# Contracting over 64 rows instead of 128 in the second score matmuls of a fused attention and mixture-of-experts kernel

## The reference: what is computed

```python
q = layernorm(x)                                     # 64 x 128 x 512, 32 heads of 16
scores  = einsum('bkgsd,bktd->bkgst', qh, kh) / 4.0  # kh, vh: the context, 8 heads of 16
weights = softmax(scores, axis=-1)
x = x + tanh(g_xattn) * einsum('bkgst,bktd->bkgsd', weights, vh)
```

## Time and profile before

| what | us |
|---|---|
| median of 3 runs | 2383.96 |
| lowest and highest run | 2383.93, 2397.22 |
| span of the profiled execution, first to last instruction | 2381.9 |
| mean granted TensorE clock over the span | 0.984 |
| first stage | about 0 to 715 |
| second stage | about 715 to 795 |
| third stage | about 795 to 2382 |

### The profile page before, as it was taken

The page is one execution under the profiler, slowest core; times in us unless marked ns, Lnnn a source line. Parts: engine busy times, 40 slices in busy tenths (PEclk is TensorE's granted clock), DMA queues, the critical chain, the costliest instruction groups (busy, mean ns, idle before and its releaser), DMA issues.

```text
span 2381.9 us, 41762 instructions
## 1 busy us (share of the span) xinstructions
PE 2290.9 (96%) x12545; PEld 1775.2 (75%) x12545; DVE 1144.9 (48%) x2214; ACT 815.7 (34%) x1426; POOL 589.5 (25%) x1378
## 2 busy tenths in 40 slices
PE   7999999999991699999999999999999999999998
PEld 5777777777771577777777777777777777777776
DVE  6999999999987422322323223232332223323232
ACT  6888888888883110101101011010110101101010
POOL 5666666666657100000000000000000000000000
PEclk9999999999995899999999999999999999999999
DMA  2444444444445422222222212322123221232211
GB/s 77 138 133 136 134 133 136 131 138 131 137 121 192 100 78 87 93 87 72 77 98 95 85 62 77 111 89 77 62 77 114 86 77 62 88 103 86 77 44 42
DMA packets 238538, 234.83 MB, mean 99 GB/s; under 512 B 88625, under 2 KB 164401, under 8 KB 238514
## 3 DMA queue, kind: packets, MB, share of 16 engines
q1 hardware_dynamic: 234162, 221.89, 29.8%
q0 software_dynamic: 4352, 12.65, 1.7%
HBM read 161.88 MB, written 71.57 MB: 98 GB/s over the span
## 4 chain that ended last, share of the span: by engine, by line
PE 66%; DVE 0%; DVEq 0%; issue 0%
PE acc L1053 7%; PE p_g L1066 7%; PE p_g L1068 7%; PE p_g L1067 7%; PE acc L1054 7%; PE acc L1055 7%; PE p_u L1068 7%; PE p_u L1067 7%; PE p_u L1066 7%; PE p_x L1096 2%; PE p_y L1083 2%; PE p_x L1083 2%; PE p_x L1074 0%; PE p_y L1089 0%; DVE keys L1036 0%; DVEq L848 0%
## 5 line engine op out<-in xcount | busy, mean ns | idle before, releaser
L997 DVE TENSOR_TENSOR act_f<-p_u,act_f 128x512 f32<-128x512 f32 x176 | 121.7, 691 | 1035.3 <-PE p_u L1068 1035.3
L968 ACT ACTIVATE act_f<-p_g 128x512 f32<-128x512 f32 x176 | 105.2, 598 | 1203.2 <-PE p_g L1068 1203.2
L530 DVE TENSOR_REDUCE negmax<-p_max 128x8 f32<-128x1024 f32 x256 | 313.1, 1223 | 66.5 <-PE p_max L672 52.0
L1053 PE MATMUL acc<-wd_h,hh 128*128 128x512 f32 x704 | 279.1, 396 | 0.0
L1066 PE MATMUL p_g<-xh,wgu_h 128*128 128x512 f32 x704 | 276.3, 392 | 1.3 <-PEq L721 1.3
L1068 PE MATMUL p_g<-xh,wgu_l 128*128 128x512 f32 x704 | 274.5, 390 | 0.0
L1067 PE MATMUL p_g<-xl,wgu_h 128*128 128x512 f32 x704 | 274.5, 390 | 0.0
L1054 PE MATMUL acc<-wd_l,hh 128*128 128x512 f32 x704 | 274.3, 390 | 0.0
L1055 PE MATMUL acc<-wd_h,hl 128*128 128x512 f32 x704 | 274.2, 390 | 0.0
L1068 PE MATMUL p_u<-xh,wgu_l 128*128 128x512 f32 x704 | 273.9, 389 | 0.0
L1067 PE MATMUL p_u<-xl,wgu_h 128*128 128x512 f32 x704 | 273.9, 389 | 0.0
(11 more groups left out here) (141 smaller groups left out, 3705.2 us busy)
## 6 DMA issues: line engine op xcount, KB each, us to landing
ew<-in_L_ffn_Wg_dram SPq DMA_DIRECT2D x32, 704.0 KB
ew<-in_L_ffn_Wu_dram SPq DMA_DIRECT2D x32, 704.0 KB
xs<-in_x_dram SPq DMA_DIRECT2D x64, 256.0 KB, 2.6
xres<-in_x_dram SPq DMA_DIRECT2D x64, 256.0 KB, 2.8
out_dram<-x SPq DMA_DIRECT2D x64, 256.0 KB, 2.0
xn_rows<-xn SPq DMA_DIRECT2D x64, 256.0 KB, 3.0
xn_cols<-xnT SPq DMA_DIRECT2D x64, 256.0 KB, 2.4
chosen<-xn_cols SPq DMA_DIRECT2D x16, 1024.0 KB, 5.6
```

What stands on the lines that cost most here:

```text
L530: nc.vector.tensor_reduce(negmax[c % 2][:, :].rearrange("p (g i) -> p i g", i=G), p_max[:, :, :].rearrange("p a (h g t) -> p (a h) g t", g ...
L1053: mm(acc[:, j, :], a[:, t], wd_h[:, f, :], start=(f == 0), stop=False)
```

## The change

Each of the two matmuls of the second pass takes only the 64 rows of its group, from both `kt` and `qt`, in place of all 128. The rows left out held zeros in `kt`, so the sums are the same. The instructions, their order, their columns, their outputs and all semaphores stay.

```diff
                             wait(pe, exp_done, 4 * b.n + c)
                             for g2 in range(2):
-                                last = mm(p_exp[:, g2, :], kt[b.par][:, c, 128 * g2:128 * g2 + 128], qt[b.par][:, c, :],
+                                half = slice(64 * g2, 64 * g2 + 64)
+                                last = mm(p_exp[:, g2, :], kt[b.par][half, c, 128 * g2:128 * g2 + 128], qt[b.par][half, c, :],
                                           start=True, stop=True)
                             last.then_inc(p2_mm, 1)
```

## The result

The changed kernel takes 2392.78 us (median of 20 runs, 2391.96 to 2403.70) where the kernel before takes 2384.34 us (median of 20): a ratio of 1.0036 with a 95% interval of 1.0026 to 1.0046, or 8 to 9 us slower. The changed kernel's profiled execution spans 2391.6 us, 9.7 us more than before. The forecast was 2398 us and "no change"; a change of 0.36% is one that this many runs can tell from nothing and that lies inside the 1% called the same.

What follows compares the result with a forecast made beforehand. PE was taken to bound the first stage. Overlapped streams, 0.10 us gaps and bare loads summed to +0.26 us a batch, +17 us, taken as +14: 2395.9 plus 2.1 gives 2398 us, range 2368 to 2440.

Steps and rivals of the forecast that it cites:

- PE's stream sets the pace of the first stage: First stage: PE busy 400.00 of 400 us, so added PE time counts in full; DVE has 9.78 us work a batch.
- The two tiles stream side by side: Second-pass pair: both 64-row matmuls share one streaming time, 0.23 us less per pair, less a 0.01 us stagger.
- Rival 2: Second-pass pairs: tiles don't stream side by side but gaps are paid; +70 us, 2454 us; chance 0.08.
- The weight loads run together: Second-pass pair: both tiles' weight loads take 0.11 us together, rather than 0.11 us more one after the other.
- Rival 3: Second-pass pairs: only the weight loads go one after the other; +42 us, 2426 us; chance 0.12.
- A gap on both sides of a pair: Entering and leaving the pair's row tiles: 0.10 us gap per change of array form, with a bare weight load behind.
- the sum: PE's block from the transpose L680 through the pair: +0.26 us a batch, +17 us, taken as +0.22 and +14 us.
- the stagger: Second-pass pair: delay of the second tile's matmul behind the first when they stream side by side, taken as 0.01 us.
- The signs that were named for it: Chunk 1 timeline: PEld empty about 0.2 us before the pair's loads; L641's load some 0.1 us after both matmuls have streamed.
- Rival 1: Second-pass pairs: changing to row tiles costs no gap, pure saving; -45 us, 2339 us; chance 0.12.
- The gain is paid back in chunks 1 and 3 only: Per chunk: +0.14 us in chunks 1 and 3; -0.01 in chunks 0 and 2, where L607's gap was already paid.
- Nobody downstream waits longer: ACT and DVE get the pair's results at 0.56 instead of about 0.58 us after the transpose, so they only gain slack.

Runs made afterwards that it cites:

- the first five runs: 64-row tiles in chunks 0/2: 0.9988; 1/3: 1.0057; each pair in one tile: 1.029; extra 8-column matmul before pairs, 128 rows: 1.0073, 64 rows: 1.0223; against the kernel before.
- run 3: Changed kernel with both matmuls of every pair on rows 0 to 63, the same 64-row tile: 2449.51 us, ratio 1.029 against the kernel before.
- runs 3 and 5: Run 3 as listed; 5 is the kernel before plus one 64-row, 8-column matmul ahead of the pair in chunks 1 and 3: 2434.36 us, ratio 1.0223.
- The two half runs: Against the kernel before, 64-row tiles in chunks 0 and 2 only: 2380.15 us, ratio 0.9988; in chunks 1 and 3 only: 2397.77 us, ratio 1.0057.
- runs 6 to 9: Kernel before, transpose of maxima moved behind value matmuls in chunks 0/2: 1.0050; plus tiles there: 1.0045; moved with SP's DMA order changed: 1.018; that plus tiles: 1.0119.

## Why the prediction was right, point by point

- *PE's stream sets the pace of the first stage.* Held: each of the first five runs moved by what its ledger of starts says, and PE is busy 400 of 400 us before and after.
- *The two tiles stream side by side.* Held: 0.50 us for both matmuls, the second of which starts 3 to 4 ns after the first in the trace, and run 3 prices the second tile at 0.23 us a pair. Rival 2, no overlap, is out.
- *The weight loads run together.* Held: both in 0.19 us. Rival 3 is out.
- *A gap on both sides of a pair.* Held, at 0.09 us (runs 3 and 5) where the sum had 0.10. The signs that were named for it are there: PEld stands empty for 0.22 us ahead of the pair, and the next line's load comes after the pair and not with it. Rival 1, no gap, is out. This is the place where the Trainium skill, TensorEngine Tiling (Array Packing), Key Properties, says that changing the mode drains TensorE: for row tiles this case's traces agree, with those 0.09 us.
- *The gain is paid back in chunks 1 and 3 only.* Held: -0.04 and +0.11 us a chunk, forecast as -0.01 and +0.14. The two half runs show the signs.
- *The size.* +8 to +9 us measured, +14 forecast. The mis-sized term is the block from the transpose to the next load: 0.66 in the sum, 0.63 in the trace. The transpose with its gap was 0.21 in the sum and is 0.20; the pair with its gap was 0.45 and is 0.43. So each of the two gaps was 0.01 too long, and the stagger, 0.01 in the sum, is 3 to 4 ns. The sum as written gave +17 us, and 0.03 x 256 = 8 us less is the 9 measured; the step from +17 to +14 was a judgement on how the gaps had been rounded, in the right direction and too small. A hundredth in a block that runs 256 times is 2.6 us, so rows with two decimals don't carry the sum further than that.
- *The batch.* It was put at 10.81 us, by counting 37 batches in 400 us; from start to start it was 10.88. It was to grow to 11.0, and is 11.03. Nothing else in the sum hangs on it.
- *What a measurement can tell.* The prediction took 1% to be about the least that could be told from nothing. With 20 runs on each side the interval is 0.1% wide to either side, so the loss is real and small, and not nothing.
- *Nobody downstream waits longer.* This holds only in that no wait downstream holds PE up: PE is busy 400 of 400 us. Taken by the word it doesn't hold: DVE's wait for `p_max` went from 23.2 to 29.4 us in the stretch, and ACT's for `p_exp` from 7.9 to 9.8. For DVE the prediction's own signs had this, by what a batch grows, and 37 x 0.15 = 5.6 us is near the 6.2 measured. It can't be taken as a licence to move things: runs 6 to 9 show how little room there is in the path of the maxima.

## What to carry to other kernels

Splitting a contraction into row tiles pays for a pair what one of its streams costs, and costs a gap on entry, a gap on exit and every weight load that was hidden across these borders. Where short pairs stand between matmuls of the full array it is a loss; where a border is there anyway, as ahead of column tiles, it is a small gain, so count borders, not tiles. Before moving an instruction to save such a border, follow the shortest path that hangs on it: here the DMAs of a maximum on SP took back more than the border would have given.

## What the runs showed of the hardware

- The gap when the array's form changes is the same for 64-row tiles as for column tiles: 0.09 us behind an 8-column transpose, behind a pair and behind a single matmul of 8 columns, beside the 0.08 to 0.11 of the earlier trace rows. It did not shrink with the size of what came before it.
- A weight load of 64 rows and 128 columns takes as long as one of 128 rows: 405.22 to 405.33, 0.11 us (run 3). Half of the rows don't make it cheaper.
- Inside one 64-row tile the next load still hides under the running matmul (405.33, run 3). Only the border takes the cover away.
